# Last stage of a graph network kernel: final rows gathered beside the joining of partition boundaries, whose 128 nodes are computed apart and scattered over the output

## The chip, the cores and the metric

One core of one Trainium2 chip. The metric is the device time of one execution in microseconds (us), median of the runs; lower is better.

## What is computed

Four graph layers in residual form over 3125 nodes with 16 features and 103125 edges; the first three are a graph convolution, a two-layer message network and a degree-normalised sum. The change touches only the fourth, an attention over the edges that enter each node, taken separately for each of 16 x 16 channels (i, o):

```python
w_m = (efeat @ W_msg + b_msg).reshape(E, 16, 16)
w_a = (efeat @ W_attn + b_attn).reshape(E, 16, 16)
h_src = feat[src][:, :, None]
e1, e2 = w_m * h_src, w_a * h_src
seg_max = segment_max(e2, dst)
ex = exp(e2 - seg_max[dst])
attn = ex / segment_sum(ex, dst)[dst]
out = x + segment_sum(e1 * attn, dst).sum(axis=1)
```

For a node the kernel needs two running sums per channel, of ex and of e1 * ex, and at the end sum over i of (second / first).

## The kernel before

The edges are sorted by destination node and dealt over 128 partitions, each with 220 steps of four slots. `attention_edges` walks them in 44 blocks of 5 steps (groups g = 0 to 4). For each step it keeps, per partition, a running maximum (`shifts`, 256 values) and the running pair of sums (`states`, 512 values), restarted where a new node begins. In a block ScalarE and VectorE multiply, ScalarE takes exponentials, VectorE weighs (`weigh`, L1984); the four slots of a group are added either by TensorE (`summed`, L1835: four matmuls with the identity into PSUM `slot_sums`) or by VectorE (`halve`, L1993, then `quarter`, L1998), and `accumulate` (L2019, L2021) adds the total to `states`. Constant BYPE = 4: groups 0 to 3 of every block go to TensorE, group 4 to VectorE. SP writes `states` and `shifts` of each block to the DRAM tables `rows_state` and `rows_shift` (L1756, L1751); the whole of the last block's `states` goes out in one DMA after its last accumulation. The row of a node's last step then holds that node's sums, except where a node's edges run over from one partition to the next.

`attention_merge` joins these. Each partition contributes its last row (`lastrow`, still in SBUF) and its head row (`heads`, the last row of its first node, gathered from `rows_state` and `rows_shift` by two indirect DMAs that POOL issues, L2156 and L2159). TensorE transposes both so that the 128 partitions lie along the free axis (`tps`, in two halves of 128 channels), VectorE runs scans along it with masks made from `flags`, ScalarE takes two exponentials, TensorE transposes back, and POOL scatters the joined sums (`outrow`, 128 rows) over the rows in `rows_state` (L2163); rows that need no joining have an index out of bounds and are dropped.

`attention_out` then runs 5 rounds of 5 tiles of 128 nodes. POOL gathers one tile per indirect DMA (`t_rows`, L2285, 25 of them, 256 KB each). Per round ScalarE takes Ln and Exp(-) of the first sums (`guess`, L2296, L2298), VectorE refines the reciprocal by one Newton step and multiplies (`error`, L2306 to L2308), reduces over i with a tensor_reduce (`o`, L2310) and subtracts from `x` in SBUF (L2313). After the last round SP writes `x` to the output in two DMAs (L2276, L2277).

Order: each of the three functions is a block of its own, and no engine enters the next block before all have left the last, SP's waits for its DMAs included. Inside a block every engine runs its own list in order, and semaphores are waited on by hand. `Masks` (run two layers earlier) prepares row numbers and flags.

## Time and profile before

| | us |
|---|---|
| median of 3 runs (2826.16 to 2830.26) | 2826.55 |
| span of the profiled execution | 2758.8 |
| edge loop starts, last accumulation ends | 1108, 2666.0 |
| joining on VectorE (first to last instruction) | 2675.9 to 2700.6 |
| first gather of final rows issued | 2705.7 |
| five rounds on VectorE | 2718.2 to 2754.2 |

The span runs from the first to the last instruction of the profiled execution; the rest of the measured time lies outside it. PE is TensorE, PEld its weight loads, DVE is VectorE, ACT is ScalarE, POOL is GpSimd, SP is SyncE; a q behind a name is the engine's sequencer, which issues DMAs. L12 is line 12. In a row, `out<-in` are the program's names, and square brackets give the idle time before the instruction and what ended it.

### The profile page before, as it was taken

The page shows a single profiled execution, that of the slowest core. Times are in us where ns is not written, and L with a number is a line of the kernel's source. Part 1 is how long each engine was busy: PE and PEld are TensorE (multiplying, and loading weights), DVE is VectorE, ACT ScalarE, POOL GpSimd, SP SyncE. Part 2 cuts the span into 40 slices and gives each one's busy share as a digit, 9 for nine tenths or more (in the row PEclk, how much of TensorE's full clock was granted, in tenths as well). Part 3 has the DMA queues.
Part 4 walks back from the last instruction along what each step waited for, and adds up shares of the span by engine and source line. Part 5 has one row for each costly group of instructions (what it writes and reads, how often), then busy time and mean ns, then how long its engine had stood idle before and what let it go on. Part 6 is the DMA issues. An engine that isn't in the chain of part 4 may idle for free. (4 is left out here: it accounts for less than half of the span.)

```text
span 2758.8 us, 36659 instructions
## 1 busy us (share of the span) xinstructions
PE 2235.6 (81%) x7911; PEld 972.4 (35%) x7912; DVE 2248.2 (81%) x3858; ACT 1731.3 (63%) x6836; POOL 1367.4 (50%) x1141
## 2 busy tenths in 40 slices
PE   1388888798699987489989999988899999988850
PEld 0144444455455543123333333333333333323320
DVE  8699999513487831399999999999999999999966
ACT  3277777301211111488888888888888888888813
POOL 6100000403551000677777777777777777777403
PEclk9599999887899998578888888887877777787875
DMA  2000000202786440112222222222222222222113
GB/s 57 18 0 0 0 0 0 92 2 84 253 259 212 151 140 23 38 53 72 71 71 71 71 71 71 71 71 71 71 71 71 71 75 75 76 76 74 65 53 101
DMA packets 105813, 205.35 MB, mean 74 GB/s; under 512 B 35333, under 2 KB 63638, under 8 KB 99998
## 3 DMA queue, kind: packets, MB, share of 16 engines
q1 hardware_dynamic: 63854, 156.28, 15.9%
q0 software_dynamic: 41904, 48.40, 8.0%
q8 instruction: 27, 0.44, 0.1%
q14 instruction: 28, 0.23, 0.0%
HBM read 76.22 MB, written 128.39 MB: 74 GB/s over the span
## 5 line engine op out<-in xcount | busy, mean ns | idle before, releaser
L1789 POOL DMA_INDIRECT hs<-h_table,gix x880 | 1132.5, 1287 | 393.4 <-issue 293.1
L1882 ACT ACTIVATE e<-wps,hs 128x32 f32<-128x32 f32 x5632 | 1020.9, 435 | 174.8 <-PE wps L1813 140.7
L1813 PE MATMUL wps<-w_edge,ef 18*128 18x512 f32 x1760 | 635.7, 805 | 201.4 <-DVE e L1919 105.4
L1835 PE MATMUL slot_sums<-e,ident 128*128 128x512 f32 x1408 | 744.0, 677 | 9.4 <-DVE e L1984 7.0
L1835 PEld LDWEIGHTS slot_sums<-e,ident 128*128 128x128 f32 x1408 | 288.1, 215 | 485.6 <-issue 444.4
L1813 PEld LDWEIGHTS wps<-w_edge,ef 18*128 18x128 f32 x1760 | 178.4, 226 | 614.2 <-ACT e L1882 255.9
L518 ACT CAST edges<-acc 128x400 f32 x600 | 295.4, 492 | 120.8 <-PE acc L505 94.6
L501 PE MATMUL acc<-q_hot,lo_hot 128*128 128x400 bf16 x1200 | 307.4, 338 | 53.7 <-DVE q_hot L475 51.5
L543 POOL DMA_INDIRECT got<-in_edge_rows,start x64 | 65.7, 1027 | 546.2 <-POOLq L456 419.9
L1919 DVE TENSOR_TENSOR e<-wps,hs 128x2048 f32<-128x2048 f32 x132 | 301.6, 2285 | 23.6 <-PE wps L1813 23.1
L475 DVE TENSOR_SCALAR q_hot<-qcol,qT 128x400 bf16<-128x400 bf16 x1200 | 290.2, 315 | 1.0 <-PE acc L505 0.9
L1892 ACT ACTIVATE e<-e 128x1024 f32<-128x1024 f32 x220 | 243.0, 1113 | 24.9 <-DVE e L1966 14.8
L1966 DVE TENSOR_TENSOR e<-e,shifts 128x1024 f32<-128x1024 f32 x220 | 256.6, 1216 | 0.0
L1984 DVE TENSOR_TENSOR e<-e 128x1024 f32<-128x1024 f32 x220 | 253.4, 1217 | 0.0
L1280 PE MATMUL acc<-edges,msg_parts 128*128 128x448 bf16 x1050 | 213.9, 359 | 18.8 <-DMA msg_parts<-msg 18.8
L505 PE MATMUL acc<-edges,ident_b 128*128 x600 | 203.2, 339 | 0.0
L1309 ACT COPY efT<-tr 128x512 f32<-128x512 f32 x56 | 32.8, 586 | 215.2 <-PE tr L1289 215.2
L501 PEld LDWEIGHTS acc<-q_hot,lo_hot 128*128 128x128 bf16 x1200 | 130.9, 140 | 93.9 <-DVE q_hot L475 68.4
L1280 PEld LDWEIGHTS acc<-edges,msg_parts 128*128 128x128 bf16 x1050 | 104.4, 100 | 109.4 <-DMA msg_parts<-msg 19.2
L1939 DVE TENSOR_TENSOR pairs<-e 128x1536 f32<-128x1536 f32 x88 | 130.5, 1483 | 5.3 <-ACT e L1882 5.2
L471 DVE TENSOR_TENSOR lo_hot<-lane,loT 128x1280 bf16<-128x1280 bf16 x120 | 98.2, 818 | 15.8 <-PE acc L505 12.1
L1948 DVE SCALAR_TENSOR_TENSOR shifts<-shifts,mk 128x256 f32<-128x256 f32 x220 | 105.9, 482 | 4.8
(372 smaller groups left out, 1952.2 us busy)
## 6 DMA issues: line engine op xcount, KB each, us to landing
rows_state<-states SPq DMA_DIRECT2D x44, 1280.0 KB, 4.5
rows_shift<-shifts SPq DMA_DIRECT2D x44, 640.0 KB, 3.0
got_order<-edges_order SPq DMA_DIRECT2D x56, 256.0 KB, 3.1
ef_order<-efT SPq DMA_DIRECT2D x56, 256.0 KB, 3.3
hs<-h_table,gix POOLq DMA_INDIRECT x880
ef<-ef_order SPq DMA_DIRECT2D x44, 320.0 KB, 3.0
edges_order<-got POOLq DMA_DIRECT2D x32, 256.0 KB, 2.6
edges_order<-msg_parts POOLq DMA_DIRECT2D x24, 256.0 KB, 3.8
```

What stands on the lines that cost most here:

```text
L475: ins = nc.vector.tensor_scalar(q_hot[:, k % HOTS, s, :], qcol[:, :], qT[:, s, at], None, ALU.is_equal)
L501: nc.tensor.matmul(total, lo_hot[:, k // HOTS % 2, :, k % HOTS * 2 + s], q_hot[:, k % HOTS, s, :], start=(s == 0), stop=False)
L518: nc.scalar.copy(edges[:, :, bass.ds(s16, W)], acc[:, k % BANKS, 0:QW].rearrange("p (t w) -> p t w", w=W)).then_inc(taken, 1)
L1280: ins = nc.tensor.matmul(acc[:, at, 0:CW], parts[:, f, k, a, :], edges[:, k, at * CW:(at + 1) * CW], start=(n == 0), stop=(n == 3 * TILES ...
L1789: nc.gpsimd.indirect_dma_start(out=hs[u][:, s, :], out_offset=None, in_=d["h_table"], in_offset=bass.IndirectOffsetOnAxis(ap=gix[u][:, s:s ...
L1813: nc.tensor.matmul(wps[:, bank, :], ef[u][k:k + KM, g * P:(g + 1) * P], w[k:k + KM, :], start=True, stop=True).then_inc(a_mult, 1)
L1835: ins = nc.tensor.matmul(sums[:, g % 2, :], ident[:, :], e[u][:, g * SLOTS + c, :], start=(c == 0), stop=(c == SLOTS - 1))
L1882: ins = nc.scalar.mul(e[u][:, s, at], wps[:, bank, at], hs[u][:, s, f:f + 1])
L1892: nc.scalar.activation(e2, e2, ACT.Exp).then_inc(a_exp, 1)
L1919: nc.vector.tensor_tensor(e[u][:, s0:s1, :].rearrange("p s (i c) -> p (s i) c", c=2 * F), wps[:, 0:s1 - s0, :].rearrange("p s (i c) -> p ( ...
L1966: nc.vector.tensor_tensor(e2, e2, bc(shift(u, g), 1, SLOTS), ALU.subtract).then_inc(a_sub, 1)
L1984: ins = nc.vector.tensor_tensor(pair[:, :, 1, :], pair[:, :, 0, :], pair[:, :, 1, :], ALU.mult)
```

## The change

In `attention_edges`: the last block has TensorE sum groups 1 and 0 only, and VectorE halves and quarters groups 2, 3 and 4. The last store of `states` is split, four groups after their accumulation and the fifth after its own. At the start of the loop SP also writes `x` to a new DRAM table `x_table`.

`attention_merge` and `attention_out` become one block. POOL issues the two head gathers, then all 25 gathers of final rows, with one of x rows (`own_x`, by the head's node number) among them. The joining runs meanwhile: the part that needs only `lastrow` first, and both channel halves in one instruction of 256 columns. Its 128 nodes no longer go back to `rows_state`. Ln and Exp of them stand among round 1's, their output rows `own_x` are computed apart, and POOL scatters these over the output (64 bytes each) once SP's output DMAs have landed. In the rounds the sum over i is made by TensorE (16 accumulating matmuls with the identity into PSUM `out_sums`), except in the last, where VectorE adds halves; `error` has two buffers, and the subtraction of round r - 1 comes after the error of round r. `Masks` keeps node numbers in place of the row number of the scatter.

```diff
+                sp.dma_start(d["x_table"].rearrange("(t p) f -> p t f", p=P), keep["x"][:, :, :]).then_inc(a_x, 16)
...
-                store_states(1, BLOCKS - 1)
+                for g0, g1 in ((0, BG - 1), (BG - 1, BG)):
+                    sp.wait_ge(a_acc, BLOCKS * BG + g1)
+                    sp.dma_start(states_t[:, (BLOCKS - 1) * BG + g0:(BLOCKS - 1) * BG + g1, :], states[1][:, g0:g1, :]
+                                 ).then_inc(a_stored[1], 16)
+                sp.wait_ge(a_x, 16)
                 for u in range(2):
                     sp.wait_ge(a_kept[u], 16 * (BLOCKS // 2))
-                    sp.wait_ge(a_stored[u], 16 * (BLOCKS // 2) + 16)
+                    sp.wait_ge(a_stored[u], 16 * (BLOCKS // 2) + 16 * (1 + u))
...
-                for u in range(2):
-                    for g in (1, 0, *range(2, BYPE)):
-                        summed(u, BLOCKS - 2 + u, g)
+                for g in (1, 0, *range(2, BYPE)):
+                    summed(0, BLOCKS - 2, g)
+                for g in (1, 0):
+                    summed(1, BLOCKS - 1, g)
...
-                for g in range(BYPE, BG):
+                for g in range(2, BG):
                     v.then(halve(1, g))
                     quarter(v, 1, g)
                 v.wait(v.n)
                 for g in range(BG):
-                    accumulate(v, 1, BLOCKS - 1, g)
+                    accumulate(v, 1, BLOCKS - 1, g, by_pe=2)
...
+            @block.gpsimd
...
+                for n in range(TILES):
+                    nc.gpsimd.indirect_dma_start(
+                        out=t[:, n, :], out_offset=None, in_=d["rows_state"],
+                        in_offset=bass.IndirectOffsetOnAxis(ap=keep["last_row"][:, n:n + 1], axis=0)
+                    ).then_inc(z_load[n // PART], 16)
+                    if n == PART:
                         nc.gpsimd.indirect_dma_start(
+                            out=own_x[:, :], out_offset=None, in_=d["x_table"],
+                            in_offset=bass.IndirectOffsetOnAxis(ap=masks.head_node[:, 0:1], axis=0)).then_inc(j_x, 16)
+                pool.wait_ge(j_row, 2)
+                pool.wait_ge(z_out, 32)
+                nc.gpsimd.indirect_dma_start(
+                    out=out, out_offset=bass.IndirectOffsetOnAxis(ap=masks.merge_node[:, 0:1], axis=0),
+                    in_=own_x[:, :], in_offset=None, bounds_check=NODES - 1, oob_is_err=False).then_inc(j_out, 16)
+                pool.wait_ge(j_out, 16)
+            @block.tensor
+            def _(pe):
...
+                for r in range(ROUNDS - 1):
+                    pe.wait_ge(z_error, r + 1)
+                    if r:
+                        pe.wait_ge(z_dve, r)
+                    some = error[:, r % 2, :, :].rearrange("p t (i o) -> p t i o", o=F)
+                    for i in range(F):
+                        ins = nc.tensor.matmul(total[:, :].rearrange("p (t o) -> p t o", o=F), ident[:, :],
+                                               some[:, :, i, :], start=(i == 0), stop=(i == F - 1))
+                    ins.then_inc(z_sum, 1)
             @block.scalar
             def _(act):
...
                 for r in range(ROUNDS):
                     act.wait_ge(z_load[r], 16 * PART)
                     if r >= 2:
+                        act.wait_ge(z_error, r - 1)
                     nc.scalar.activation(ratio(r), rows(r)[:, :, 0, :], ACT.Ln).then_inc(z_ln, 1)
+                    if r == 1:
+                        act.wait_ge(j_row, 1)
+                        nc.scalar.activation(chan(own_guess[:, :]), pair(outrow[:, :])[:, :, 0, :], ACT.Ln
+                                             ).then_inc(j_guess, 1)
                     act.wait_ge(z_ln, r + 1)
                     nc.scalar.activation(ratio(r), ratio(r), ACT.Exp, scale=-1.0).then_inc(z_guess, 1)
+                    if r == 1:
+                        act.wait_ge(j_guess, 1)
+                        nc.scalar.activation(own_guess[:, :], own_guess[:, :], ACT.Exp, scale=-1.0).then_inc(j_guess, 1)
             @block.vector
             def _(dve):
+                v = Line(dve, j_dve)
...
+                v.add(nc.vector.tensor_scalar(diag[:, 0, :], ident[:, :], masks.flags[:, 0:1], None, ALU.mult))
+                v.add(nc.vector.tensor_scalar(diag[:, 1, :], ident[:, :], masks.flags[:, 1:2], None, ALU.mult))
+                flatten(0, lastrow)
+                dve.sem_inc(j_last, 1)
...
+                v.then(nc.vector.tensor_copy(cols[:, 0, :, :], turned[:, 0, :, :]))
+                last_sh = cols[:, 0, 0, :]
+                v.then(nc.vector.tensor_tensor_scan(sh[:, :], mask[:, 0, :], last_sh, 0.0, ALU.add, ALU.max))
+                v.add(nc.vector.tensor_tensor(tmp[:, 0, :], last_sh, sh[:, :], ALU.subtract))
+                v.then(nc.vector.tensor_tensor(tmp[:, 1, 1:TWO], sh[:, 0:TWO - 1], mask[:, 0, 1:TWO], ALU.add))
+                nc.vector.tensor_tensor(tmp[:, 1, 1:TWO], tmp[:, 1, 1:TWO], sh[:, 1:TWO], ALU.subtract).then_inc(j_in, 1)
+                dve.wait_ge(j_heads, 32)
+                flatten(1, heads)
+                dve.sem_inc(j_flat, 1)
+                dve.wait_ge(j_exp, 1)
...
+                def corrected(value, off, guessed):
+
+                    v.then(nc.vector.tensor_tensor(off, value[:, :, 0, :], guessed, ALU.mult))
+                    v.then(nc.vector.scalar_tensor_tensor(off, off, 2.0, guessed, ALU.subtract, ALU.mult))
+                    return nc.vector.tensor_tensor(off, off, value[:, :, 1, :], ALU.mult)
+                def round_error(r):
                     dve.wait_ge(z_guess, r + 1)
+                    if r >= 2:
+                        dve.wait_ge(z_sum, r - 1)
+                    off = error[:, r % 2, :, :].rearrange("p t (i o) -> p (t i) o", o=F)
+                    corrected(rows(r), off, ratio(r)).then_inc(z_error, 1)
+                def nodes(r):
+                    return x[:, r * PART:(r + 1) * PART, :]
+                def round_sum(r):
+                    dve.wait_ge(z_sum, r + 1)
+                    nc.vector.tensor_tensor(nodes(r), nodes(r), total[:, :].rearrange("p (t o) -> p t o", o=F),
+                                            ALU.subtract).then_inc(z_dve, 1)
+                round_error(0)
+                dve.wait_ge(j_row, 1)
+                dve.wait_ge(j_guess, 2)
+                dve.wait_ge(j_x, 16)
+                v.then(corrected(pair(outrow[:, :]), chan(own[:, :]), chan(own_guess[:, :])))
+                v.then(nc.vector.tensor_reduce(own_o[:, :], own[:, :].rearrange("p (i o) -> p o i", o=F), X, ALU.add))
+                nc.vector.tensor_tensor(own_x[:, :], own_x[:, :], own_o[:, :], ALU.subtract).then_inc(j_row, 1)
+                for r in range(1, ROUNDS):
+                    round_error(r)
+                    round_sum(r - 1)
+                dve.wait_ge(z_error, ROUNDS)
+                some = error[:, (ROUNDS - 1) % 2, :, :]
+                v.then(nc.vector.tensor_tensor(half[:, :, :], some[:, :, 0:CH // 2], some[:, :, CH // 2:CH], ALU.add))
+                width = CH // 4
+                while width >= F:
+                    v.then(nc.vector.tensor_tensor(half[:, :, 0:width], half[:, :, 0:width], half[:, :, width:2 * width],
+                                                   ALU.add))
+                    width //= 2
+                last = nodes(ROUNDS - 1)
+                nc.vector.tensor_tensor(last, last, half[:, :, 0:F], ALU.subtract).then_inc(z_dve, 1)
```

## Rows read from the trace of the kernel before

**Rows 1.** The chain that ended last, in pieces: start us, us, what.

```profile
2710.69 3.56 DMA t_rows<-rows_state,last_row
...
2753.93 0.24 DVE x_sb L2313
```

**Rows 2.** Groups of instructions, 2704 to 2760; busy us, mean ns, idle before.

```profile
L2285 POOL DMA_INDIRECT t_rows<-rows_state,last_row x25 | 26.3, 1052 | 10.4 <-issue 7.3 <-PEq L2272 3.1
...
L2310 DVE TENSOR_REDUCE o<-error 128x80 f32<-128x1280 f32 x5 | 11.5, 2296 | 0.2
...
L2306 DVE TENSOR_TENSOR error<-t_rows,guess 128x1280 f32<-128x1280 f32 x5 | 7.5, 1504 | 17.7 <-ACT guess L2298 17.5
...
L2296 ACT ACT_TABLE_LOAD x5 | 6.4, 1283 | 10.3 <-PEq L2153 10.2
...
L2296 ACT ACTIVATE guess<-t_rows 128x1280 f32<-128x1280 f32 x5 | 6.3, 1270 | 15.3 <-DMA t_rows<-rows_state,last_row 15.3
```

**Rows 3.** Timeline at the end of the edge loop: start us, us, instruction, idle before.

```profile
2651.53 1.23 DVE L1993 TENSOR_TENSOR e<-e 128x1024 f32<-128x1024 f32 x1
...
2652.78 0.69 DVE L1998 TENSOR_TENSOR e<-e 128x512 f32<-128x512 f32 x1
...
2656.43 0.69 DVE L2019 TENSOR_TENSOR states<-states,slot_sums 128x512 f32<-128x512 f32 x1 [2.96 <-PE slot_sums L1835]
...
2665.26 0.75 DVE L2021 SCALAR_TENSOR_TENSOR states<-states,mk,e 128x512 f32<-128x512 f32 x1
...
2666.04 0.33 SPq L1756 DMA_DIRECT2D rows_state<-states  x1
```

**Rows 4.** DMA issues, 2640 to 2760: KB each, median us to landing.

```profile
rows_state<-states SPq DMA_DIRECT2D x2, 1280.0 KB, 4.5
...
t_rows<-rows_state,last_row POOLq DMA_INDIRECT x25, 3.7
...
rows_state<-outrow,merge_rows POOLq DMA_INDIRECT x1, 2.7
```

**Rows 5.** Timeline of the joining.

```profile
2671.64 0.94 POOL L2156 DMA_INDIRECT heads<-rows_state,merge_rows  x1 [80.91 <-SPq L2153]
...
2675.93 0.29 DVE L2194 COPY flat<-lastrow 128x256 f32<-128x256 f32 x1 [9.26 <-DMA heads<-rows_shift,merge_rows]
...
2679.21 2.67 PE L2174 MATMUL tps<-ident,flat 128*128 128x128 f32 x12
...
2681.99 1.76 DVE L2204 COPY cols<-tps 128x1536 f32<-128x1536 f32 x1 [2.11 <-PE tps L2174]
...
2683.78 0.42 DVE L2207 TENSOR_TENSOR_SCAN sh<-mask,cols 128x128 f32<-128x128 f32 x1
...
2699.93 0.69 DVE L2240 COPY outrow<-mops 128x512 f32<-128x512 f32 x1 [1.26 <-PE mops L2179]
...
2701.52 1.03 POOL L2163 DMA_INDIRECT rows_state<-outrow,merge_rows  x1 [27.69 <-DVE outrow L2240]
```

**Rows 6.** Timeline of POOL in the last rounds: a gather alone, one beside VectorE.

```profile
2714.44 0.95 POOL L2285 DMA_INDIRECT t_rows<-rows_state,last_row  x1 [0.30 <-issue]
...
2722.36 1.22 POOL L2285 DMA_INDIRECT t_rows<-rows_state,last_row  x1 [0.30 <-issue]
```

**Rows 7.** Timeline of TensorE elsewhere: short f32 matmuls at two clocks.

```profile
560.85 1.77 PE L871 MATMUL small<-w,agg 48*128 48x64 f32 x14
...
614.58 3.17 PE L888 MATMUL small<-w,agg 64*128 64x16 f32 x14
```

**Rows 8.** Windows: us, busy of each engine, granted TensorE clock, DMA share, GB/s.

```profile
560.00:570.00 10.00, 10.00 (x86) 6.10 (x83) 4.36 (x7) 0.00 (x0) 0.00 (x0) 1.00 0.01 2
...
610.00:620.00 10.00, 10.00 (x37) 6.72 (x36) 1.23 (x6) 1.93 (x4) 0.00 (x0) 0.50 0.00 0
...
2681.40:2682.00 0.60, 0.48 (x3) 0.18 (x1) 0.01 (x1) 0.00 (x0) 0.00 (x0) 0.80 0.00 0
```

**Rows 9.** Timeline of VectorE at the start of the edge loop.

```profile
1135.79 0.18 DVE L1930 CAST gix<-src_order 128x20 int32<-128x20 int16 x1 [25.05 <-DMA hs<-h_table,gix]
```

## What the time after should be

> **What bounds the kernel now.** I read the end of the span backwards. The chain of work that ended last begins with the gathers of final rows: the fifth lands 3.56 us after its issue at 2710.69, and from there ScalarE and VectorE carry the chain to 2754.17 [rows 1]. The groups of that stretch show why. Five rounds of VectorE work take 3 x 1.5 + 2.3 + 0.3 = 7.2 us each, without gaps, and VectorE had been idle for 17.7 us before the first, because nothing of a round could start until the joining had written its rows back [rows 2]. So the last stage is a string: store, heads, joining (25 us of many small VectorE instructions), scatter, gathers, five rounds, output. The timeline of the stretch before it shows a second string, at the end of the edge loop: VectorE has waited 2.96 us for TensorE's slot sums at 2656.43, and its five accumulations of 0.75, waiting again and again, last until 2666.0 [rows 3]. The profiled execution spans 2758.8 us; the median of the runs shown is 2826.55, so 67.75 us lie outside the span, and I carry them over unchanged.
>
> All times below stand on the clock of the profile before.
>
> **Slot sums of the last block.** TensorE sums two groups in place of four; VectorE halves and quarters three groups in place of one. A halving takes 1.23 us and a quartering 0.69 [rows 3], and with their overlap a group costs about 1.92, so VectorE is done at 2651.53 + 3 x 1.92 = 2657.3. TensorE's first two sums were ready at 2656.4, where the first accumulation started, so the five accumulations then run without a wait: 5 x 0.8 = 4.0, end at 2661.3 in place of 2666.0 [rows 3]. Gain 4.7.
>
> **Split store.** It waits for that last accumulation. Before: issue at 2666.04, 4.5 us to landing for 1280 KB [rows 3, 4]. After: four rows go at 2660.5, the last quarter megabyte at 2661.3. Nothing shows such a DMA. It lies between the 256 KB scatter's 2.7 and the whole store's 4.5 [rows 4], so it lands from 2664.0 to 2665.8; I take 2664.6, nearer to the scatter, whose size it has. Heads were issued about 1.1 us after the landing (2671.64 against 2670.5 [rows 3 to 5]); so now POOL starts at about 2665.8 and the other engines, which wait for nothing there, at about 2665.4. The x_table wait on SP has only these store waits behind it.
>
> **Gathers.** POOL now issues 2 + 25 + 1 descriptor instructions in one run from 2665.8, with no scatter and block change between. Issues follow at 1.25 us when VectorE is quiet and at 1.52 beside its 1280-element instructions, 1.05 busy on the mean [rows 2, 6]; I take 1.25 for the first fourteen and 1.40 after. With 3.7 to land [rows 4], the five rounds' rows are there at 2677.0, 2684.5, 2691.2, 2698.2 and 2705.2.
>
> **Joining.** It now handles 256 columns in one instruction where it had two of 128, and the half that needs no heads starts at once. Prices: 128-column scan 0.42, 128x512 instruction 0.69, 1536-column copy 1.76, twelve transposes 2.67, outrow copy 0.69 [rows 3, 5]. Thus scan of 256 about 0.69, other 256-column instructions 0.42, copy of 768 about 0.95, six transposes 1.3. In order: diag and flat 0.9; mask product and transposes 2.7; copy 0.95; scan and three instructions 1.95; flat of the heads 0.65 (they land at 2670.1, 4.3 after their first issue as before [rows 5], so no wait); Exp wait 0.15; weights 0.69, two scans 1.4, one sum 0.45; copy 0.95; three instructions 1.3; Exp 0.8; three of 512 2.1; transposes 1.3; outrow 0.69. Sum 17.0, end at 2682.4. Before it was 2675.93 to 2700.6, 24.7 [rows 5]. Four microseconds before its end ScalarE is free.
>
> **Rounds.** ScalarE pays 1.28 for a table, 1.27 for Ln, 1.28 and 1.27 for Exp [rows 2]: 5.1 a round. Round 0: free at 2678.5, guess at 2683.6, error (three instructions, 4.55 with gaps) to 2688.1. The 128 nodes ride on round 1's tables, so no load is added: two activations of 0.6, their guess at 2689.8 (its Ln waits for outrow, 2682.4, which is long there). VectorE waits for that 1.7, then 2.2 for the nodes' own chain, to 2692.0; queued behind this wait is error 1. Error 1 ends at 2696.6.
>
> The 2.3 us reduction is now 16 accumulating 128x80 matmuls on TensorE, 32 passes as f32 splits into two (each weight load has two records before). Nothing before has this shape. The nearest rows: 14 passes of 64 columns in 1.77 where the granted clock was 1.00 (2.4 GHz), 0.12 each, and 14 of 16 columns in 3.17 where it was 0.50 (1.2 GHz), 0.22 each [rows 7, 8]. So a sum costs 4.0 to 7.4. TensorE was idle and at 0.50 before the transposes of the joining, and 0.80 over their last 0.6 us [rows 8]; a sum should start at the low level and get part of the high one. I take 5.5, the middle. It hides behind the next round's error unless it exceeds it. VectorE pays 0.3 for the subtraction. Then:
> round 2: guess 2695.1, error 2696.9 to 2701.4; sum 1 ends 2702.3, subtraction to 2702.8;
> round 3: guess 2702.1, error 2702.8 to 2707.3; sum 2 to 2708.4, subtraction to 2708.7;
> round 4: rows 2705.2, Ln, table, Exp: guess 2709.1, error to 2713.6; sum 3 to 2714.3, subtraction to 2714.6.
> The last sum is a tree on VectorE: 640, 320, 160, 80 elements, about 0.83, 0.48, 0.32, 0.24, and a subtraction of 0.25: 2.3 with gaps. VectorE ends at 2716.9 in place of 2754.17. What is late last is then mixed: gathers, ScalarE's 3.8 behind them, and TensorE's sums, all within two microseconds of each other.
>
> **Output.** From VectorE's end to the span's end 4.6 as before (2754.17 to 2758.8) [rows 1]. New behind it: the scatter of 128 rows over the output, which may start only when the output has landed. The scatter of before cost 0.9 from its release to its start (2700.62 to 2701.52) and 2.7 to land [rows 4, 5]; 3.7 in all, nothing hides it, nothing is queued behind it but the end. These rows are 64 bytes, not 2 KB, so it could be a microsecond less.
> End: 2716.9 + 4.6 + 3.7 = 2725.2, 33.6 less.
>
> **At nothing.** The store of x to x_table (3200 runs of 64 bytes, the output's layout, under 4.6 us) goes out on SP while ScalarE and VectorE wait 25 us for the first gathers [rows 9]; SP's next instruction waits for those too. Without that cover, 4.6. Two small VectorE copies of node numbers: under 0.3, taken as zero.
>
> **Two rules of the Trainium skill.** A table load stands before every Ln and before every Exp, five each [rows 2]. The Trainium skill, "ScalarE: Activation LUTs", section "Table sets: the hidden batching unit", says that one set holds both and one load serves ln then exp. The trace disagrees. By that rule the sum above would end 1.6 earlier, as an estimate.
> The other rule speaks against the change, and is the slow rival below.
>
> **Rivals.**
> (a) TensorE's sums stay at the low level, 7.4 each. They then follow one another, since each needs the one PSUM bank freed by the subtraction: sum 1 to 2704.4, sum 2 to 2712.2, sum 3 to 2720.0; end 2730.9, 27.9 less, 2798.6 us. For it: rows of small f32 matmuls at 0.50 [rows 8]. Against: the rise in the joining.
> (b) Slower: gathers starve beside the joining. POOL's issue was 22% slower beside VectorE's two-input instructions [rows 6]; the gathers now stand beside nothing else. If the pitch doubled to 2.5 us, the last rows land at 2737, and the end is at 2756, level; it turns slower by over 0.2% from 2.8 us a gather on, where the time is about 2832. Against: over the 25 gathers, most of them beside VectorE's rounds, busy time and issue gaps came to 1.34 each [rows 2].
> By the Trainium skill, "GPSIMD Engine Reference", section "Key points", GpSimd shares its SBUF interfaces with VectorE and contends with instructions that have two SBUF inputs. The trace agrees in kind, with the 1.25 and the 1.52.
> (c) The overlap does not come: first guesses late, rounds still 7 us each after the joining's end. From 2682.4: 5.1 + 5 x 6.9 = 2722, and 8.3 for the output plus 2.2 for the nodes' own chain, 2732.5: 2800 us.
>
> **How the numbers follow.** Forecast 2826.55 - 33.6 = 2793 us, chance 0.72; (a) 0.15; (c) 0.08; (b) and whatever else is slower 0.03; level 0.02. The low end is sums at 4.0 (0.7 less), the store's early bound (0.6), a cheaper scatter (1) and the joining 2 shorter: 2788. The high end takes in (a) and (c) with the store's late bound (1.2) and a gather pitch of 1.5 throughout (2): 2804. That leaves out (b) and mishaps of the first sort that add over 10. A difference under 0.2% (5.6 us) can't be told from none here; faster by more 0.95, within 0.02, slower 0.03.
>
> **What would show it.** In the profile after: last accumulation near 2661; heads at 2666; outrow within 18 us of the block's start; 28 POOL descriptor instructions at 1.25 to 1.5; sums of 32 passes in 4 to 7.4; VectorE's waits for them under 1.5 each; one scatter of 3.7 after the output. Wrong would be: a sum over 9 us, POOL's pitch over 2, rounds that start only after outrow has been worked on for long, or an edge loop whose blocks take another time than before, for which I see no reason.

## The result and the profile after

| | before | after |
|---|---|---|
| median of the runs, us | 2828.11 (2826.16 to 2830.26) | 2807.78 (2806.35 to 2812.15) |
| profiled span, us | 2758.8 | 2804.6 |
| from the last block's scaling to the end of the span, us | 122.6 | 103.5 |
| TensorE clock granted, mean over the span | 0.83 | 0.84 |

The ratio of the times is 0.9924, 95% interval 0.9912 to 0.9936: faster by 20.3 us, where 33.6 had been forecast, and outside the forecast range. The two spans can't be compared as they stand; why is the first thing that the experiments settle. The stretch that the change touches can: it begins for both kernels with the scaling of the edge loop's last block (`scale` on VectorE), and it is 19.1 us shorter. All that follows is read in it. "The stretch" below is this one, "before" and "after" are the two kernels, and "late" is the time from the end of TensorE's last pass of a sum to its signal that the sum is done. The stretch starts 64.92 us later in after than in before, so a step of the forecast, which stands on the clock of before, is compared with the trace of after less 64.92.

The timeline of after, in pieces (start us, us, engine, line, operation, idle time before it and what ended it). First the end of the edge loop and the start of the joining:

```profile
2722.16 0.69 DVE L2027 TENSOR_TENSOR states<-states,slot_sums 128x512 f32<-128x512 f32 x1
...
2723.80 2.46 DVE L2029 SCALAR_TENSOR_TENSOR states<-states,mk,e 128x512 f32<-128x512 f32 x3
2725.44 1.19 SPq L1782 DMA_DIRECT2D rows_state<-states  x2
...
2731.11 1.21 POOL L2199 DMA_INDIRECT heads<-rows_state,merge_rows  x1 [78.73 <-POOLq L1739]
```

The accumulations run without a wait and end at 2726.26, on the clock of before 2661.3, where they ended at 2666.0 [rows 3]. POOL starts at 2666.2 in place of 2671.64 [rows 5]. The joining and the first rounds:

```profile
2746.45 0.69 DVE L2322 COPY outrow<-mops 128x512 f32<-128x512 f32 x1 [1.21 <-issue]
...
2748.39 1.49 DVE L2329 TENSOR_TENSOR error<-t_rows,guess 128x1280 f32<-128x1280 f32 x1 [1.25 <-ACT guess L2266]
```

Outrow is done at 2747.14, 16.7 us after the first instruction of the joining; before it took 24.7 [rows 5]. Then the rounds:

```profile
2752.99 7.12 PE L2246 MATMUL out_sums<-error,ident 128*128 128x80 f32 x32 [6.58 <-issue]
...
2760.24 1.49 DVE L2331 TENSOR_TENSOR error<-error,t_rows 128x1280 f32<-128x1280 f32 x1
...
2767.87 0.94 POOL L2206 DMA_INDIRECT t_rows<-rows_state,last_row  x1 [0.30 <-issue]
2769.57 0.24 DVE L2347 TENSOR_TENSOR x_sb<-x_sb,out_sums 128x80 f32<-128x80 f32 x1 [7.84 <-remote]
...
2777.08 0.24 DVE L2347 TENSOR_TENSOR x_sb<-x_sb,out_sums 128x80 f32<-128x80 f32 x1 [2.82 <-PE out_sums L2246]
...
2777.46 7.09 PE L2246 MATMUL out_sums<-error,ident 128*128 128x80 f32 x32 [0.42 <-DVE x_sb L2347]
...
2784.59 0.24 DVE L2347 TENSOR_TENSOR x_sb<-x_sb,out_sums 128x80 f32<-128x80 f32 x1 [2.81 <-PE out_sums L2246]
...
2792.09 0.24 DVE L2347 TENSOR_TENSOR x_sb<-x_sb,out_sums 128x80 f32<-128x80 f32 x1 [2.81 <-PE out_sums L2246]
```

Two things are to be seen. The first subtraction (L2347) waits 7.84 us for a sum whose last pass had ended at 2760.11; by its own record TensorE's signal comes 9.4 us after that. The profile records when a pass starts and models when it ends; the 32 passes start 0.21 apart to the last, so a late signal and a last pass that ended late can't be told apart here. And from there on a subtraction comes every 7.5 us: a sum of 7.09, 0.42 until TensorE starts the next, VectorE waiting 2.8 each time. The rounds, which VectorE used to set at 7.2 each [rows 2], are now set by TensorE at 7.5, and only the joining has come out of the string. Its clock in two of the sums (us, busy of PE, of PEld, ..., granted clock, DMA share, GB/s):

```profile
core 0: us, PE busy (x), PEclk, DMA share, GB/s
2753.00:2760.10 7.10, 7.10 (x32) 0.50 0.63 182
2770.00:2777.00 7.00, 7.00 (x32) 0.50 0.09 33
```

The granted clock is 0.50 (1.2 GHz) in both. The chain of work that ended last shows the end (start us, us, what):

```profile
2794.26 0.25 DVE x_sb L2369
2794.53 0.39 SPq L2193
...
2794.97 3.73 DMA out<-x_sb
...
2799.64 1.03 POOL out L2216
```

From VectorE's end, 2794.50, to the end of the span it takes 10.1 us; before it was 4.6 [rows 1].

### The profile page after: what moved, and what is told of

Same layout as the page of the kernel before. It is cut to its first block and busy times, and to the rows that moved or that the text cites. A ratio compares the mean times of both kernels' runs of the same rounds, so it can differ in the third digit from the quotient of the medians.

```text
span 2804.6 us, 36863 instructions
## 1 busy us (share of the span) xinstructions
PE 2222.7 (79%) x8023; PEld 987.6 (35%) x8024; DVE 2242.8 (80%) x3841; ACT 1744.7 (62%) x6838; POOL 1340.9 (48%) x1142
## 5 line engine op out<-in xcount | busy, mean ns | idle before, releaser
L1796 POOL DMA_INDIRECT hs<-h_table,gix x880 | 1103.6, 1254 | 483.6 <-issue 311.1
L1890 ACT ACTIVATE e<-wps,hs 128x32 f32<-128x32 f32 x5632 | 1033.7, 405 | 226.2 <-PE wps L1820 145.1
L1820 PE MATMUL wps<-w_edge,ef 18*128 18x512 f32 x1760 | 578.0, 707 | 300.4 <-ACT e L1890 144.6
L1842 PE MATMUL slot_sums<-e,ident 128*128 128x512 f32 x1392 | 760.3, 697 | 8.5 <-DVE e L1992 7.0
L1842 PEld LDWEIGHTS slot_sums<-e,ident 128*128 128x128 f32 x1392 | 295.8, 224 | 491.4 <-issue 466.1
L1820 PEld LDWEIGHTS wps<-w_edge,ef 18*128 18x128 f32 x1760 | 158.8, 200 | 677.0 <-ACT e L1890 295.7
L1310 ACT COPY efT<-tr 128x512 f32<-128x512 f32 x56 | 32.8, 586 | 214.9 <-PE tr L1290 193.6
```

Source lines behind the costliest of these rows:

```text
L1796: nc.gpsimd.indirect_dma_start(out=hs[u][:, s, :], out_offset=None, in_=d["h_table"], in_offset=bass.IndirectOffsetOnAxis(ap=gix[u][:, s:s ...
L1820: nc.tensor.matmul(wps[:, bank, :], ef[u][k:k + KM, g * P:(g + 1) * P], w[k:k + KM, :], start=True, stop=True).then_inc(a_mult, 1)
L1842: ins = nc.tensor.matmul(sums[:, g % 2, :], ident[:, :], e[u][:, g * SLOTS + c, :], start=(c == 0), stop=(c == SLOTS - 1))
L1890: ins = nc.scalar.mul(e[u][:, s, at], wps[:, bank, at], hs[u][:, s, f:f + 1])
```

## The experiments

The theories. **A:** the forecast was right up to the first sum, and missed because the sums take 7.1 us in place of 5.5 and follow one another, because TensorE's first signal comes late, and because the scatter at the end costs more. **B** (near the forecast's rivals of starved gathers and of an overlap that does not come): the gathers, or what they do to the engines beside them, took the gain back. **C:** the edge loop became slower, since its blocks in the two profiles differ. The table gives for each kernel the stretch from the last block's scaling to the end of the span, which one profile shows to some 0.8 us (the two of after differ by that), and the time where several runs were made, as a ratio to runs of the kernel before on the same chip.

| kernel | stretch, us | ratio (95%) |
|---|---|---|
| before, again (e0) | 122.4 | 1.0000 (0.9983 to 1.0017) |
| after, again (e4) | 102.8 | 0.9941 (0.9924 to 0.9958) |
| trees on VectorE (e1) | 96.0 | 0.9905 (0.9873 to 0.9937) |
| gathers held for the first sum (e2) | 104.9 | 0.9938 (0.9917 to 0.9958) |
| sums of 4 x 320 columns (e3) | 94.6 | 0.9888 (0.9852 to 0.9924) |
| sums of 8 x 160 columns (e5) | 94.3 | 0.9909 (0.9881 to 0.9937) |
| gathers behind the joining (e6) | 108.8 | |
| no scatter (e7) | 100.0 | |
| pause in the gathers (e8, e11) | 102.4, 101.8 | |
| slot sums of before (e9) | 103.0 | |
| uneven rounds (e10) | 93.8 | 0.9878 (0.9862 to 0.9895) |

**The kernel before, again.**

> The kernel before, unchanged, profiled once more. In the profile of before a block of the edge loop takes 34.13 us; in the profile of after 34.6, 35.1 and 36.0 in turn. Theory one: the profiled execution of before was one with a quicker loop than its timed runs, and nothing lay outside its span: then this profile has a span of about 2824.5 us (2826.5 less the 1.75 that lie outside the span of after), and blocks of about 35.3. Theory two: 67 us lie outside the span of before: then the span is again about 2759, beside a time of about 2827.

Theory one. The span is 2813.6 and the run's time 2815.38, so 1.8 us lie outside the span. The scaling of the first and of the last block, in the first profile of before and in this one (the first two lines are of the former):

```profile
1167.07 0.48 DVE L1970 SCALAR_TENSOR_TENSOR scale<-shifts,mk 128x256 f32<-128x256 f32 x1
...
2636.16 0.48 DVE L1970 SCALAR_TENSOR_TENSOR scale<-shifts,mk 128x256 f32<-128x256 f32 x1
```

```profile
1189.33 0.48 DVE L1970 SCALAR_TENSOR_TENSOR scale<-shifts,mk 128x256 f32<-128x256 f32 x1
...
2691.18 0.48 DVE L1970 SCALAR_TENSOR_TENSOR scale<-shifts,mk 128x256 f32<-128x256 f32 x1
```

22.3 us are lost in the first block, and 32.8 over the 43 after it, whose lengths go from 34.2 to 36.0 in a sawtooth, as in after, and were 34.1 in the first profile but for the first and the last two. Together 55, which is the difference of the spans (54.8) but for 0.2. So the first profile of before was of a quicker execution than any run that was timed, and theory C falls: on this chip a block takes 34.93 us on the mean here (1501.85 by 43) and 34.94 in e1, e2 and e3, which have the changed kernel's loop. The store of x to x_table does not show either: in e1, e2 and e3, which have it, the first block's scaling starts at 1188.6, 1192.2 and 1189.6, and here at 1189.3. What the first block looks like in both is in the windows from 1136 (PE, PEld, DVE, ACT, POOL busy and instructions, clock, DMA share, GB/s), first of the quick execution:

```profile
1136.00:1150.00 14.00, 11.14 (x31) 3.72 (x32) 4.58 (x2) 14.00 (x80) 10.61 (x12) 0.50 0.07 8
```

```profile
1136.00:1150.00 14.00, 4.16 (x10) 1.01 (x10) 2.47 (x2) 5.99 (x29) 10.41 (x11) 0.50 0.07 8
```

and in the timeline of ScalarE in this one:

```profile
1152.68 0.29 ACT L1882 ACTIVATE e<-wps,hs 128x32 f32<-128x32 f32 x1 [1.11 <-issue]
1154.08 0.29 ACT L1882 ACTIVATE e<-wps,hs 128x32 f32<-128x32 f32 x1 [1.11 <-issue]
...
1165.97 2.25 ACT L1882 ACTIVATE e<-wps,hs 128x32 f32<-128x32 f32 x12 [0.41 <-issue]
```

ScalarE starts an activation about every 1.40 us, waiting for nothing that the profile shows, while POOL issues gathers and for some 4 us after the last of them; from 1165.97 on it starts one every 0.19. But in the quick execution POOL issued as many gathers in the same 14 us (12 against 11), and ScalarE made 80 activations beside them: gathers alone do not make it slow. I come back to this.

**The changed kernel, again.**

> The changed kernel, unchanged, profiled once more. VectorE's wait of 7.84 us before the first subtraction, for a signal that TensorE gave 9.4 us after its last pass, ended 0.75 us after the last gather had been issued. Theory one: the code and the gathers beside it fix the wait: it is there again, between 6 and 9 us, and from the last block's scaling to the end the span takes 103.5 us as in after. Theory two: it is an accident of that execution: it is under 1 us here, and the stretch is 95.7 us.

Theory one: the wait is there again, 6.93 us, and the stretch is 102.8.

**The sums on VectorE.**

```diff
-                    dve.wait_ge(z_sum, r + 1)
-                    nc.vector.tensor_tensor(nodes(r), nodes(r), total[:, :].rearrange("p (t o) -> p t o", o=F),
-                                            ALU.subtract).then_inc(z_dve, 1)
+                    v.then(nc.vector.tensor_tensor(half[:, :, :], some[:, :, 0:CH // 2], some[:, :, CH // 2:CH],
+                                                   ALU.add))
...
+                    nc.vector.tensor_tensor(nodes(r), nodes(r), half[:, :, 0:F], ALU.subtract).then_inc(z_dve, 1)
```

> The changed kernel, but each round's sum is the halving tree on VectorE that the last round has; TensorE does none. Theory one: the five rounds of after were bound by TensorE's sums (7.1 us and 0.42 for the subtraction, one after another), and the 7.84 us that VectorE waited at 2761.73 were TensorE's late signal. Then VectorE needs 4.5 + 2.3 = 6.8 a round, without a wait: from 2757.3 four errors and five trees, 29.7, end at 2787 where it was 2794.5: 7.5 less, about 2800 us. Theory two: the 7.84 us belong to VectorE or to the memory that it writes, and not to TensorE: then a gap of that length shows among the trees, and the time is about 2808, as after.

Theory one, to the number: 7.5 us less than in after. VectorE has no wait from round 1 on, and rounds come every 6.62 us:

```profile
2754.37 1.48 DVE L2320 TENSOR_TENSOR error<-t_rows,guess 128x1280 f32<-128x1280 f32 x1
...
2758.82 0.82 DVE L2338 TENSOR_TENSOR error_half<-error 128x640 f32<-128x640 f32 x1
...
2760.99 1.48 DVE L2320 TENSOR_TENSOR error<-t_rows,guess 128x1280 f32<-128x1280 f32 x1
```

So sums on TensorE, as the change has them, cost more than trees on VectorE; their rounds of 7.5 are no shorter than the 7.2 of before, with its reductions of 2.3. The gathers beside the rounds are nearly the same here (1.43 us apart, 1.36 in after), so what they do to VectorE did not take the gain; of theory B it stays open whether they made TensorE's first signal late.

**Fewer, wider matmuls.**

```diff
-                    for i in range(F):
+                    for i in range(0, F, 4):
+                        ins = nc.tensor.matmul(total[:, :, :, :], ident[:, :], some[:, :, i:i + 4, :],
+                                               start=(i == 0), stop=(i == F - 4))
...
+                    v.then(nc.vector.tensor_reduce(four_o[:, :, :], total[:, :, :, :].rearrange("p t i o -> p t o i"),
+                                                   X, ALU.add))
```

> The changed kernel, but a sum is 4 accumulating matmuls of 320 columns in place of 16 of 80, and VectorE adds the four that are left (a reduction of 320 elements, about 0.5 us) before it subtracts. In after a pass of 80 columns starts every 0.213 us and one of 16 columns took 0.22 in the trace of before. Theory one: a pass costs a fixed 0.21 and up to 320 columns little more: then a sum is 8 passes, 1.8 to 2.4 us, is hidden behind an error, and the rounds are bound by VectorE at 4.5 + 0.9 = 5.4 or by the gathers: VectorE ends near 2783, 11 less, about 2797 us. Theory two: the columns set the price: a sum is again about 7 us, and the time about 2808 or 2 more for the reductions. If the late signal is of the gathers it may stay, at up to 7.8 in the first case.

The stretch is 9 us shorter than in after. The four sums, in windows (PE busy, clock, DMA share, GB/s):

```profile
2744.30:2748.80 4.50, 4.50 (x8) 0.50 0.63 180
2753.70:2757.70 4.00, 4.00 (x8) 0.59 0.49 145
2758.80:2761.10 2.30, 2.30 (x8) 1.00 0.65 166
2765.40:2769.90 4.50, 4.50 (x8) 0.50 0.00 0
```

Neither theory has the price, which depends on the clock. Eight passes take 4.6 at 0.50 and 2.4 at 1.00, so 320 columns cost 0.57 and 0.30 a pass, more than the fixed 0.21 and less than four passes of 80. That is enough to hide a sum behind an error. Now the gathers bound the end: VectorE waits for the guess of round 4, which waits for its rows.

```profile
2768.95 1.49 DVE L2330 TENSOR_TENSOR error<-t_rows,guess 128x1280 f32<-128x1280 f32 x1 [3.73 <-ACT guess L2267]
```

By its stretch this kernel beats both. By its time it beats before; against after the time does not decide, since the intervals touch.

**Eight matmuls of 160** (the edit of e3 with `range(0, F, 2)`), **and no scatter.**

> The changed kernel, but a sum is 8 accumulating matmuls of 160 columns in place of 16 of 80, and VectorE adds the two that are left: half the TensorE instructions of after, twice those of the kernel with 4 of 320, in which no signal came late. Theory one: TensorE's instructions run out while gathers are being issued, after a certain number of them (one sum of after, 64 with the weight loads): then the second sum here is the one whose signal comes late, until about 0.75 us after the last gather. Theory two: the first sum is late whatever it is made of: then the first subtraction waits again, 4 us or more. Theory three: neither, no wait over 2 us for a sum beside the gathers. The price of a sum: 16 passes, by 0.213 a pass 3.4 us, by the columns (0.50 to 0.58 for 320) 4.3 to 4.6; hidden behind an error of 4.55 either way. Without a late signal the time is as with 4 of 320 (within 2 us).

The sums took 4.0, 4.3, 2.4 and 4.6 us, the first at a granted 0.59, the third at 1.00, the fourth at 0.50; no wait of VectorE's for a sum, which is theory three. But the first signal, by its own record, came at 2763.99, 3.3 us after the last pass, hidden behind error 1; the second at once, though gathers stood beside it until 2775. So it is the first sum that is late, but by less; and theory one's count of instructions, by which it would be the second, falls.

```diff
-                pool.wait_ge(z_out, 32)
-                nc.gpsimd.indirect_dma_start(
-                    out=out, out_offset=bass.IndirectOffsetOnAxis(ap=masks.merge_node[:, 0:1], axis=0),
...
```

> The kernel with sums of 8 matmuls of 160 columns, but the 128 nodes of partition boundaries are not scattered over the output at the end (so these rows of the output are not the final ones). The forecast put the scatter at 3.7 us. In after it takes 5.5: from VectorE's end to the end of the span 10.1 us, where before it was 4.6. Theory one: 5.5 less from VectorE's end to the end. Theory two (the forecast): 3.7 less, because the output itself lands later here.

The kernel that ran was the changed kernel itself with its 16 matmuls, without the scatter, not the one with 160 columns that this names; for the price that makes no difference. From VectorE's end, 2794.72, to the end of the span, 2799.3, it takes 4.6. So the scatter costs 5.5 us, theory one. The first signal was late by 10.9 here.

**The gathers behind the joining.**

```diff
+                pool.wait_ge(j_row, 1)
                 for n in range(TILES):
```

> The changed kernel, but the gathers of final rows wait for the joined rows, so they no longer run beside the joining: they start 13.3 us later. Theory one: the overlap is what the change gains, and all 13.3 us come back: from the last block's scaling to the end 116.8 us in place of 103.5. Theory two: the rounds of after were bound by the four sums on TensorE and by the late signal, so part of the overlap was wasted: worked through with sums of 7.1 and rows that come 1.36 us apart, VectorE ends 7.5 us later and the stretch is 111, if no signal is late; with the first signal held until the last gather up to 14 later.

Nearer to theory two: 108.8. The gathers of final rows start 13.5 us later, and the stretch is only 5 to 6 longer. First error and first subtraction:

```profile
2762.89 1.52 DVE L2330 TENSOR_TENSOR error<-t_rows,guess 128x1280 f32<-128x1280 f32 x1 [12.79 <-ACT guess L2267]
...
2777.90 0.23 DVE L2348 TENSOR_TENSOR x_sb<-x_sb,out_sums 128x80 f32<-128x80 f32 x1
```

The first signal came at 2777.26, 2.6 us after the last pass and 8.7 before the last gather had been issued, so a late signal does not last until the gathers end. Here it is hidden behind error 1. From the scaling to the first subtraction it takes 73.8 us, in after 68.5, and from there both go on at 7.5 a round. But after's subtraction had waited 7.84 for its late signal. Without that wait the two would lie 13.2 apart, nearly the 13.5 of the gathers: the overlap was worth its full length, and the late signal of after ate more than half of it.

**The slot sums of before.**

```diff
-                for g in (1, 0):
-                    summed(1, BLOCKS - 1, g)
+                    for g in (1, 0, *range(2, BYPE)):
+                        summed(u, BLOCKS - 2 + u, g)
...
-                for g in range(2, BG):
+                for g in range(BYPE, BG):
```

> The changed kernel, but the last block's slot sums are those of before: TensorE four groups, VectorE one (the store stays split). Theory one: this part gains what the traces say, 4.7 us from the start of the last block's scaling to the last accumulation; then it is 29.7 here, as in before, where it was 25.2 in after, and the end comes 4.5 us later, 108 us from the scaling. Theory two: the split store gave part of it, and what comes behind makes up for the rest: then 105 or less.

From the scaling to the copy behind the last accumulation it takes 29.9 us, in after 25.2: theory one for the part itself, 4.7. The stretch is none the longer, because the first signal is less late here: by 4.2 us, where it was 9.4 in after:

```profile
2750.33 0.24 DVE L2346 TENSOR_TENSOR x_sb<-x_sb,out_sums 128x80 f32<-128x80 f32 x1 [2.60 <-remote]
```

**What makes the first signal late.** Three kernels were for this.

```diff
                 for n in range(TILES):
+                    if n == 2 * PART:              (e2)
+                        pool.wait_ge(z_sum, 1)
+                    if n == 6:                     (e8, e11)
+                        pool.wait_ge(j_row, 1)
...
                 round_error(0)
+                round_sum(0)                       (e11)
```

> The changed kernel, but the gathers of rounds 2 to 4 wait for the signal of the first sum, so none is being issued while the first sum runs. Theory one: the signal comes late (9.4 us after the last matmul) because the gathers are being issued, or because their rows are moving: then it comes within 0.2 us of the last matmul here, VectorE's wait of 7.84 is gone, and a stall moves to the second sum, which now runs beside the gathers. Theory two: it comes late for a reason of TensorE's own (the first use of this code, its place): then 7.8 us stay before the first subtraction, and the gathers of rounds 2 to 4 start about 2769.6. Either way rows come later: the last gather ends near 2781 by theory one and near 2790 by theory two, and the time is 2808 to 2812 or about 2818.

> The changed kernel, but the seventh gather of final rows waits for the joined rows, so POOL issues none for some 5 us before the first sum begins; the gathers go on beside the sum as in after. Where no gather stood beside the first sum its signal came at once, beside gathers it came 9.4, 8.7 and 10.9 us late with 16 matmuls and 3.3 with 8. Theory one: TensorE gets its further instructions late while gathers are being issued; in a pause ahead of the sum it gets them, so the first signal is on time (within 0.5 us of the last pass) or much less late, though gathers stand beside it: no wait at the first subtraction, VectorE ends about 3 us earlier than in after, and from the last block's scaling to the end it takes about 100 us. Theory two: gathers beside the sum itself hold the signal up, whatever went before: late by 8 us or more, and the stretch takes 106 to 109.

> As the kernel with the pause in the gathers ahead of the first sum, but VectorE subtracts the first sum straight after error 0, before the nodes of the partition boundaries, so that its wait shows when the first signal comes (in the kernel with the pause alone that wait was covered). The sum's 32 passes take 7.12 us and VectorE starts to wait when they start. Theory one: in the pause TensorE gets the instructions that it lacked, and the signal is on time: VectorE waits 7.1 to 7.6 us. Theory two: gathers beside the sum hold the signal up: VectorE waits 9.5 us or more (late by 2.6 to 10.9 in the runs that showed it).

With no gather beside the first sum the signal came at once (2753.52, last pass 2753.51), and the second sum, now beside the gathers, was on time too: of the first expectation theory one holds for the first sum, and its moved stall does not come. The rows came late in exchange (VectorE waits 12.4 us for the guess of round 2), so the stretch is no shorter than in after. With the pause alone (e8), VectorE had no wait at the first subtraction, but the subtraction came 7.2 us after the last pass, too late to tell. With the subtraction put first (e11):

```profile
2744.43 7.12 PE L2248 MATMUL out_sums<-error,ident 128*128 128x80 f32 x32 [6.57 <-DVE error L2333]
```

```profile
2746.74 0.94 POOL L2208 DMA_INDIRECT t_rows<-rows_state,last_row  x1 [0.30 <-issue]
...
2751.58 0.24 DVE L2349 TENSOR_TENSOR x_sb<-x_sb,out_sums 128x80 f32<-128x80 f32 x1 [7.21 <-issue]
```

The signal is on time, with gathers issued all along the sum. The pause, 4.84 us, had ended 5.6 us before the sum began. All that is known of the first sum:

| kernel | gathers beside it | ahead of it | late, us |
|---|---|---|---|
| after, e4, e7 | yes | yes | 9.4, 8.7, 10.9 |
| e9 | yes | yes | 4.2 |
| e5 (half the matmuls) | yes | yes | 3.3 |
| e6 | yes | yes | 2.6 |
| e11 | yes | yes, with a pause of 4.8 us | 0.0 |
| e2 | none | yes, then 5 us without | 0.0 |
| e10 (a quarter of the matmuls; below) | yes | yes | 0.0 |

In e3, also with a quarter of the matmuls, VectorE first needed the signal 3.9 us after the last pass and did not wait. No later sum whose signal is on record was late by more than 0.7.

So what is shown is this. With 16 or 8 matmuls a sum, a long run of gathers ahead of TensorE's first use of this code goes with a late signal, by an amount that varies; a break of 5 us shortly ahead of the sum goes with none, and so do 4 matmuls a sum without any break, in one execution each. That TensorE lacked instructions, which came late while gathers were issued, would fit this, and ScalarE's 1.40 us an activation in the first block of the loop looks like the same thing. But the profile has no row of an instruction that is waited for, and what it has speaks against it. It counts the packets that move instructions, on two queues. Here are the queues of after in the 8 us up to the late signal, and in the 30 behind (packets, MB, share of 16 engines):

```profile
q0 software_dynamic: 472, 1.54, 66.5%
```

```profile
q8 instruction: 1, 0.02, 0.2%
q14 instruction: 2, 0.02, 0.2%
```

From 2732 to 2777 no packet of instructions moved, only gathers, and the signal came at 2769.55; the next three packets lie between 2777 and 2782, in the third sum. If instructions were late, it was not for a packet that the trace counts. The cause stays open.

**A version that uses this.** Wide sums, rounds of 7, 7, 6, 3 and 2 tiles, the output stored in two, the boundary nodes last.

> The kernel with sums of 4 matmuls of 320 columns, with three things more: the rounds have 7, 7, 6, 3 and 2 tiles in place of five each, the first twenty tiles of the output are stored as soon as they are done, and the 128 nodes of partition boundaries are fetched after the final rows and computed last, beside the output's store. With five equal rounds VectorE had to wait 1.4 and 3.7 us for the guesses of rounds 3 and 4, whose rows came late, and from the last Ln to VectorE's end it took 11.3 us. Theory one: gathers bound the end now; then the smaller last rounds shorten that stretch to about 8, the fetch moved away gives 1.25 and the smaller last store about 1: from the last block's scaling to the end 89 to 91 us where it was 94.6, a time ratio to before of about 0.986. Theory two: the end is bound by VectorE and its sums, whatever the sizes: 93 to 95.

Theory two: 93.8, and the time is that of the kernel with equal rounds, within the intervals; this one's interval lies below that of after, so it beats both kernels. What follows the last round is 2 us shorter, 8.1 from VectorE's last subtraction, but that comes 1.1 later: the sum of round 2 takes 5.4 us, and error 4 waits for it.

```profile
2762.45 0.56 DVE L2353 TENSOR_REDUCE four_o<-out_sums 128x96 f32<-128x384 f32 x1 [2.72 <-PE out_sums L2252]
```

## Why the prediction was wrong, step by step

**Right, and to half a microsecond.** On the clock of before: last accumulation forecast 2661.3, measured 2661.3; POOL's start 2665.8 and 2666.2; the joining 17.0 us and 16.7, its end 2682.4 and 2682.2; guess 0 2683.6 and 2683.4; error 0 2688.1 and 2688.0; the nodes' chain 2692.0 and 2692.4; error 1 2696.6 and 2696.8. So the slot sums (4.7, shown again by e9), the split store, the joining's prices from neighbouring rows and the cover of x_table's store all held. The gathers came every 1.36 us on the mean (28 issues from 2731.11 to 2767.87), inside the forecast's 1.25 to 1.40; the slow rival (b) did not happen. By the Trainium skill, "GPSIMD Engine Reference", section "Key points", GpSimd contends with VectorE instructions of two SBUF inputs; the trace agrees: a gather kept POOL busy for 0.95 alone and up to 1.96 beside them in e3.

**Wrong: the price of a sum.** The step "I take 5.5, the middle" put between 4.0 and 7.4, on the ground that the clock had risen in the joining's transposes. The clock stayed at 0.50 and a sum took 7.1, 0.22 a pass, close to the high bound, to which the nearest row at 0.50 [rows 7, 8] had pointed. The middle was chosen where the row to lean on was the one of the stretch's own clock. The rise to 0.80 was a window of 0.6 us at the end of twelve transposes [rows 8]; the changed kernel makes them in two sixes of 1.5 us, and from 2726.1 to 2804 its granted clock is 0.50 throughout. Each sum then exceeds the error of 4.5 that should hide it, and since each needs the PSUM bank freed by the subtraction they stand in a row. From error 1 to VectorE's end it is 32.8 us in place of 20.3: 7.84 for the late signal, and the rest, 4.6, for the sums. The sums are rival (a), to which I gave 0.15 and 27.9 us of gain.

**Wrong: nothing late in the handing over.** "VectorE's waits for them under 1.5 each" had no case in which TensorE's signal comes later than its work. That is the 7.84, the larger part of the 8.8 between rival (a)'s gain and the 19.1 measured, and no row of before has such a wait in the last stage. Why the signal is late stays open.

**Wrong: the scatter at 3.7.** It costs 5.5 (e7). The 3.7 was release to landing in the middle of the kernel; at the end 10.1 us stood behind VectorE in place of the forecast's 8.3.

Sum: 7.84 + 4.6 + 1.8 = 14.2, of the 14.5 between the 33.6 forecast and the 19.1 measured in the stretch.

**Wrong, without effect on the gain: the 67.75 us outside the span.** Nothing lies there but 1.8 us; the profile of before was of a quicker execution (e0). The gain came out of a stretch that is the same in both profiles of before, 122.6 and 122.4, so the reading did no harm, but the difference of span and median was a sign that should have been followed into the loop.

## What to carry to other kernels

Work that is moved to an idle engine to save a short step becomes the bound if the idle engine needs longer for it than the step beside it: price it at the clock that the engine has in that stretch, and put the price against what is to hide it. For an accumulation by unit-matrix matmuls, try few wide passes and a short finish on VectorE: here they beat many narrow ones by 9 us in five rounds. And where a profile's span is 2% off the timed runs, find the stretch that differs before using its durations.

## What the runs showed of the hardware

An f32 pass on TensorE of 80 columns took 0.213 us at a granted 0.50; of 160 columns 0.29 at 0.50 and 0.15 at 1.00; of 320 columns 0.57 and 0.30. The granted clock went to 1.00 in the third sum of e3 and e5, which started 1.1 and 0.8 us after the one before had ended, and was back at 0.50 in the fourth, after 4.2 and 4.1 us of idleness; in after, where sums stand 0.42 apart, it stayed at 0.50. And engines can be slow to go on though nothing in the profile holds them: ScalarE at 1.40 us an activation of 0.29 in e0's first block, TensorE's first signal 2.6 to 10.9 us late in six executions. POOL was issuing gathers in both, but it did so too where ScalarE was quick and where the first signal came at once (e10, e11). An indirect scatter of 128 rows of 64 bytes as the last step added 5.5 us (e7).
